# Two graph-attention layers, eight batches: rows of two stages spread by TensorE instead of through memory, exponentials issued ahead of the next normalisation, and a regrouped opening and ending

## What is computed

```python
h = relu(layernorm(x))                     # over the 128 features
Wh = h @ W                                 # [1024, 128]
e[i, j] = leaky_relu(Wh[i] @ a1 + Wh[j] @ a2, slope 0.2)
att = softmax over j of where(adj[i, j] > 0, e[i, j], -large)
x = x + elu(att @ Wh)                      # layer 0
x = x + att @ Wh                           # layer 1, with its own W and a
```

## Time and profile before

| | |
|---|---|
| median of 3 executions | 315.14 us (313.93 to 317.64) |
| profiled execution, its own time | 314.74 us |
| its span in the trace | 312.9 us |
| TensorE matmul busy | 293.6 us, 94% of the span |
| VectorE / ScalarE / GpSimd busy | 267.3 / 164.5 / 47.6 us |
| row_r from memory, 15 loads | 3.9 us each from issue to landing, median |

### The profile page before, as it was taken

How to read it: one execution, slowest core, us unless ns; L and a number is a source line. 1 busy time by engine, 2 the same in 40 slices (tenths; PEclk the granted TensorE clock), 3 DMA queues, 4 the chain that set the end, 5 groups by cost and what they waited for, 6 DMA issues and landing times.

```text
span 312.9 us, 6581 instructions
## 1 busy us (share of the span) xinstructions
PE 293.6 (94%) x2560; PEld 288.6 (92%) x2560; DVE 267.3 (85%) x610; ACT 164.5 (53%) x485; POOL 47.6 (15%) x53
## 2 busy tenths in 40 slices
PE   7999779799899999999999999999999999789695
PEld 7899679799899999999999999999999999788595
DVE  4596389949999989999899989999899959919785
ACT  3284480784493747483583648382674654353200
POOL 2612001220303030303003030303002000400000
PEclk9999999999999999999999999999999999999999
DMA  7997495102574334904574345713491302001211
GB/s 248 410 405 317 154 389 197 67 2 68 190 244 175 138 134 151 384 7 142 195 310 162 138 135 189 284 68 115 161 356 47 138 0 70 0 0 40 96 69 67
DMA packets 15247, 50.56 MB, mean 162 GB/s; under 512 B 2040, under 2 KB 3056, under 8 KB 15216
## 3 DMA queue, kind: packets, MB, share of 16 engines
q1 hardware_dynamic: 14640, 49.75, 43.0%
q10 hardware_dynamic: 576, 0.39, 0.4%
HBM read 45.88 MB, written 4.26 MB: 160 GB/s over the span
## 4 chain that ended last, share of the span: by engine, by line
PE 74%; DVE 10%; DMA 4%; ACT 4%; issue 4%; POOL 2%; POOLq 0%; DVEq 0%; ACTq 0%
PE acc L790 55%; PE prj L750 7%; PE tp L693 4%; DVE pbuf L564 4%; DMA row_r<-r_rows 3%; PE acc L806 2%; PE acc L690 2%; ACT xn L349 2%; POOL rstd L254 2%; DMA r_rows<-rT 1%; DVE stats L476 1%; DVE x_sb L594 1%; DVE ex L588 1%; PE prj L753 1%; DVE accs L573 1%
## 5 line engine op out<-in xcount | busy, mean ns | idle before, releaser
L790 PE MATMUL acc<-wh,pbuf 128*128 128x129 f32 x1984 | 232.9, 276 | 10.1 <-DVE accs L573 8.1
L790 PEld LDWEIGHTS acc<-wh,pbuf 128*128 128x128 f32 x1984 | 227.0, 192 | 13.3 <-issue 9.9
L564 DVE SCALAR_TENSOR_TENSOR pbuf<-row_r,sqr,adj_sb 128x1024 f32<-128x1024 f32 x127 | 157.8, 1278 | 8.8 <-DMA row_r<-r_rows 8.8
L254 POOL TENSOR_TENSOR rstd<-vareps,neg_half 128x8 f32<-128x8 f32 x15 | 37.5, 2503 | 213.9 <-DVE vareps L494 213.8
L379 ACT ACTIVATE accs<-accs,rec 128x128 f32<-128x128 f32 x120 | 36.7, 390 | 59.3 <-DVE rec L583 59.3
L349 ACT ACTIVATE xn<-x_sb,shift,rstd 128x128 f32<-128x128 f32 x120 | 47.6, 480 | 0.0
L368 ACT ACTIVATE wh<-prj,wh 128x128 f32<-128x128 f32 x120 | 31.6, 350 | 0.0
L750 PE MATMUL prj<-w_ext,hT 128*128 128x130 f32 x240 | 29.4, 275 | 0.1
L750 PEld LDWEIGHTS prj<-w_ext,hT 128*128 128x128 f32 x240 | 28.0, 191 | 0.2 <-ACT hT L355 0.2
L573 DVE TENSOR_TENSOR accs<-acc,uniform 128x387 f32<-128x387 f32 (+1 forms) x48 | 22.0, 508 | 4.2 <-PE acc L790 2.0
L476 DVE BATCH_NORM_STATS2 stats<-x_sb 128x6 f32<-128x128 f32 x120 | 24.6, 279 | 0.0
(11 more groups left out here) (81 smaller groups left out, 146.1 us busy)
## 6 DMA issues: line engine op xcount, KB each, us to landing
adj_sb<-in_adj SPq DMA_DIRECT2D x64, 512.0 KB, 6.5
row_r<-r_rows SPq DMA_DIRECT2D x15, 512.0 KB, 3.9
x_sb<-in_x SPq DMA_DIRECT2D x7, 512.0 KB, 7.1
out_x<-x_sb SPq DMA_DIRECT2D x7, 512.0 KB, 3.0
out_x<-x_sb SPq DMA_DIRECT2D x2, 192.0 KB, 1.9
x_sb<-in_x ACTq DMA_DIRECT2D x1, 256.0 KB, 3.6
x_sb<-in_x SPq DMA_DIRECT2D x1, 256.0 KB, 3.4
r_rows<-rT SPq DMA_DIRECT2D x15, 4.0 KB
```

The source lines that it names most:

```text
L254: nc.gpsimd.tensor_tensor(rstd[:, :], vareps[:, :], neg_half[:, :], ALU.pow).then_inc(rstd_ready, 1)
L564: nc.vector.scalar_tensor_tensor(pbuf[:, t, :], row_r[:, n % 2, :], sqr[:, n % 2, 0, t:t + 1], adj_at(b, t), ALU.max, ALU.min).then_inc(p_ ...
L790: mm = nc.tensor.matmul(acc[:, k, s * C:(s + 1) * C], pbuf[:, t, i * P:(i + 1) * P], wh[:, n % 2, t, :], start=(t == 0 and s == 0), stop=( ...
```

## The change

1. **Rows of stages 1 and 15** (`SPREAD`) no longer go through memory. TensorE spreads them by 8 transposes (`spread_r`) in the place of `turn_r`, and ScalarE copies them to `row_r` in two halves (`copy_row`). The mask tiles of batch 2 are issued without a wait for row 1, and x of batches 4 and 5 goes behind `load_row(2)`.
2. **ScalarE's order.** In the stage before a LATE one, `copy_hT(n+1)` goes ahead of `scale_accs(n-1)`, and `exps(n+1)` with the row's copy ahead of `normalise(n+2)`. In stage 0 `normalise(2)` goes ahead of `exps(1)`. The very first exponentials are split: row values first, the two others after them.
3. **Opening.** Warm-up counts 24, 6, 4, 3 become 20, none, 2, 3 (the second entry of the new tuple is not used). W a of layer 0 is computed after the first four transposes, that of layer 1 after the first projection. Six of the eight statistics of batch 1 are issued ahead of `copy_e_first`, two behind it.
4. **VectorE's order.** The masks issued ahead of `take_acc` are 4 for stage 1, 1 for stage 3, 3 for stage 13 and 2 otherwise. The statistics of stages 3, 5 and 15 are moved: those of 3 and 15 ahead of the mask tiles 7 and 6 to 7 of the stage before, those of 5 from the head of stage 3 to the place behind `exp_args(4)`.
5. **TensorE's order around LATE stages.** In stage 2 `transposes(3)` follows two tiles instead of one, then one tile, then `project(3)`; in stage 14 `transposes(15)` follows one tile, then one tile, then `project(15)`. In stages 1 and 13 `turn_r` stands one tile later.
6. **Ending.** The last output tile goes to a bank of its own (`LAST_TILE`, in `prj`), which ScalarE first fills with the `uniform` row (`seed_last`); the ending has four parts (3, 3, 1 and 1 tiles), and the last is read from PSUM without a copy.

```diff
+    SPREAD = (1, LAST)
+    last_parts = [(0, NB), (NB, 2 * NB), (2 * NB, T - 1), (T - 1, T)]
+        LAST_TILE = prj[:, 0, 0:C]
+        def before_drain(n):
+            return {1: 4, AHEAD: 1, LAST - 2: 3}.get(n, 2)
...
@@ SyncE
-            for m in range(1, AHEAD):
-                for t in range(T):
-                    load_adj(m, t)
-                load_x(m + 2)
-                load_row(m)
-                sp.wait_ge(row_in, 16 * m)
-            load_x(AHEAD + 2)
+            for t in range(T):
+                load_adj(1, t)
+            load_x(3)
+            for t in range(T):
+                load_adj(2, t)
+            load_row(2)
+            load_x(4)
+            load_x(5)
             load_row(AHEAD)
...
@@ ScalarE
+            def copy_row(m):
+                k = spread_rows(m)
+                for h in range(2):
+                    act.wait_ge(row_spread, 2 * k + h + 1)
+                    cols = slice(h * (N // 2), (h + 1) * (N // 2))
+                    nc.scalar.activation(row_r[:, m % 2, cols], tp[:, cols],
+                                         ACT.Copy).then_inc(row_copied, 1)
+            def seed_last():
+                act.wait_ge(wh_ready, T * LAST + T)
+                act.wait_ge(e_copied, 3 * LAST + 3)
+                nc.scalar.activation(LAST_TILE, uniform[:, LAST % 2, :],
+                                     ACT.Copy).then_inc(seeded_last, 1)
...
+            normalise(2)
+            exps(1)
+            scale_wh(1, range(3))
+            copy_row(1)
+            scale_wh(1, range(3, T))
+            copy_hT(2)
+            for n in range(1, LAST + 1):
+                elu = stages[n - 1][0] == 0
                 if n + 1 in LATE:
                     copy_hT(n + 1)
+                scale_accs(n - 1)
+                if n + 1 in LATE or n + 2 in LATE:
                     elu_exp(n - 1) if elu else None
+                if n < LAST:
                     exps(n + 1)
+                    if n + 1 in SPREAD:
+                        copy_row(n + 1)
+                    else:
+                        copy_r(n + 1)
+                    if n + 1 not in LATE and n + 2 not in LATE:
+                        elu_exp(n - 1) if elu else None
+                    if n + 2 <= LAST and n + 2 not in LATE:
+                        normalise(n + 2)
                     scale_wh(n + 1)
                 if n + 2 in LATE:
                     normalise(n + 2)
                 elif n + 2 <= LAST:
                     copy_hT(n + 2)
+            seed_last()
...
@@ TensorE
+            def spread_r(m):
+                pe.wait_ge(sqr_ready, m + 1)
+                for t in range(T):
+                    mm = nc.tensor.transpose(tp[:, t * P:(t + 1) * P],
+                                             sqr[:, m % 2, 2, t:t + 1].to_broadcast([P, P]),
+                                             ident[:, :])
+                    if t % 4 == 3:
+                        mm.then_inc(row_spread, 1)
...
+                        if t == 0 and n == LAST and i == T - 1:
+                            pe.wait_ge(seeded_last, 1)
...
                 if n + 1 in LATE:
-                    attend(n, (0,))
+                    k = 1 if n + 1 in SPREAD else 2
+                    attend(n, range(k))
                     transposes(n + 1)
-                    attend(n, (1, 2))
+                    attend(n, (k,))
                     project(n + 1)
-                    attend(n, (3,))
+                    attend(n, (k + 1,))
                     spread_emax(n + 1)
-                    attend(n, (4,))
-                    turn_r(n + 1)
-                    attend(n, (5,))
+                    attend(n, (k + 2,))
+                    spread_r(n + 1) if n + 1 in SPREAD else turn_r(n + 1)
+                    attend(n, range(k + 3, 6))
                 else:
                     project(n + 1)
                     attend(n, (0,))
                     spread_emax(n + 1)
-                    attend(n, (1,))
+                    attend(n, (1, 2) if n + 2 in LATE else (1,))
                     turn_r(n + 1)
-                    attend(n, (2, 3, 4, 5))
+                    attend(n, (3, 4, 5) if n + 2 in LATE else (2, 3, 4, 5))
                 if n + 2 <= LAST and n + 2 not in LATE:
                     transposes(n + 2)
                 attend(n, (6, 7))
```

More of the change, by code:

```diff
@@ L160, in gat_two_layers @@
         x1_ready = sem("x1_ready")
+        seeded_last = sem("seeded_last")
         last_ready = sem("last_ready")
@@ L172, in adj_at, with spread_rows, loaded_rows @@
             return adj_sb[:, s:s + N]
+        def before_drain(n):
+            return {1: 4, AHEAD: 1, LAST - 2: 3}.get(n, 2)
+        def spread_rows(m):
+            return len([k for k in SPREAD if k < m])
+        def loaded_rows(m):
+            return len([k for k in range(1, m + 1) if k not in SPREAD])
         def xn_before(m):
@@ L363, in exps, with scale_wh @@
                 nc.scalar.mul(wh[:, m % 2, :, D], sqr[:, m % 2, 1, :], Q_SCALE).then_inc(q_ready, 1)
-            def scale_wh(m):
+            def scale_wh(m, tiles=range(T)):
                 act.wait_ge(q_ready, m + 1)
-                for t, (k, s) in enumerate(bank_of):
+                for t in tiles:
+                    k, s = bank_of[t]
                     nc.scalar.activation(wh[:, m % 2, t, 0:D], prj[:, k, s * E:s * E + D],
@@ L409, in _ @@
             scale_wh_first(range(T - 1, T))
[L410 to L413, removed]
+            normalise(2)
[6 more added lines that the diff above has]
+                elu = stages[n - 1][0] == 0
                 if n + 1 in LATE:
                     copy_hT(n + 1)
+                scale_accs(n - 1)
+                if n + 1 in LATE or n + 2 in LATE:
                     elu_exp(n - 1) if elu else None
-                    normalise(n + 2) if n + 2 <= LAST else None
+                if n < LAST:
                     exps(n + 1)
[L419 to L428, removed]
-                if n < LAST:
+                    if n + 1 in SPREAD:
[6 more added lines that the diff above has]
+                        normalise(n + 2)
                     scale_wh(n + 1)
@@ L464, in statistics_first, with statistics_second @@
                                             ALU.add, ALU.max).then_inc(xn_dve, 1)
+            def statistics_second(tiles):
+                src = x3_at(1)
+                if tiles[0] == 0:
+                    dve.wait_ge(x_in[1], 16)
+                    dve.wait_ge(vareps_ready, 1)
+                    nc.vector.memset(gate[:, :], 0.0)
+                for t in tiles:
+                    st = nc.vector.bn_stats(stats[:, t, :], src[:, t, :])
+                if tiles[-1] == T - 1:
+                    st.then_inc(bn_done, 1)
             def statistics(m):
@@ L641, in _ @@
                 l, b = stages[n - 1]
-                if n + 2 <= LAST and n + 2 not in LATE and n + 1 not in LATE:
+                if n + 2 <= LAST and not {n, n + 1, n + 2} & set(LATE):
                     statistics(n + 2)
                     moments(n + 2)
-                masks(n, (0, 1))
+                masks(n, range(before_drain(n)))
                 take_acc(n - 1)
@@ L678, in _ @@
                     masks(n, (6, 7))
-            masks(LAST, (0, 1))
+            masks(LAST, range(before_drain(LAST)))
             take_acc(LAST - 1)
@@ L836, in _ @@
             attend(0, (4,))
-            turn_r(1)
+            spread_r(1)
             attend(0, (5, 6))
```

194 lines of the change are left out of this document (129 added, 65 removed).

## The result

The changed kernel takes 305.81 us (median of 4, 305.2 to 306.9); the kernel before took 314.53 beside it. The ratio is 0.9709, 95% interval 0.9664 to 0.9754. The profiled execution of the changed kernel took 305.33 us with a span of 303.5. Forecast were 303.9 and a span of 301.7.

The account below looks back on a forecast made before the run. TensorE, busy 94%, bounds the kernel; only its waits in stages 1-3 and 13-15 can go. Stage 4 -6.1, stages 13 and 14 -2.1 - 4.5, seed +2.1, ending -0.6: -11.2, giving 303.9 us, range 299.8 to 307.8.

Parts of the forecast that it names:

- norms come late: Rival, chance 0.17: opening gives nothing, shifts locked out in stages 3 and 13 (+0.9), `exps(1)` waits 0.8; 306.6 us.
- Opening: Before stage 0: fewer first transposes and split exponentials start stage 0 1.7 us earlier, 1.0 of it kept.
- the rival of the slow clock: Rival, chance 0.03: TensorE stays at 1.2 GHz into stage 0; a whole stage 0 so would give 321 us.
- The old waits of 1.95 and 2.98 us: TensorE's waits before stages 1 and 15, where VectorE's masks waited for the row from memory; forecast to go.
- the rival by which VectorE's own work keeps them: Rival, chance 0.05: in stages 1 and 15 VectorE's work replaces the row as bound, both waits stay; about 309 us.
- lands at 47.6: Stage 1: row 2, written at 42.5, lands at 47.6, before VectorE is ready for it at 47.8.
- First new wait: Stage 2: TensorE waits 2.0 us at `transposes(4)`, since ScalarE does stage 3's exponentials and row copy before `normalise(4)`.
- 1.6 us given back by the sum: Stage 3: moved statistics of stage 5 delay mask 3 (+1.1 with the handover), and the accumulators come late (+0.5).
- the first free gap: Stages 3 and 14: GpSimd's shift gets in at the first gap among VectorE's masks; otherwise 0.2 and 0.7 late.
- The 0.5 that I had put on the accumulators of stage 3: Start of stage 4: VectorE takes stage 3's accumulators from 91.9, TensorE comes at 92.0 and starts at 92.5, +0.5.
- Second new wait: Stage 15, first tile: TensorE waits 2.0 to 2.1 us for `seed_last`, issued by ScalarE behind `scale_accs(14)`.
- Stages 13 and 14, ending: Stages 13 and 14 gain 2.1 and 4.5 us as old waits go; the smaller last part gains 0.6.

Follow-up runs that it names:

- five repairs: Changed kernel with seed, transposes and statistics repairs, stage 2's second mask behind the accumulators, x of batches 4 and 5 ahead of row 2: 299.38 us.
- three repairs: Changed kernel with the seed ahead of the scaling, stage 4's transposes one tile later, stage 5's statistics at the head of stage 3: 299.42 us.
- second experiment: Changed kernel with the transposes of stage 4 one tile later in stage 2: 304.91 us.
- third: Changed kernel with the statistics of stage 5 back at the head of stage 3: 304.82 us.
- sixth experiments: Changed kernel with VectorE waiting in stage 3 for GpSimd's shift of stage 5, before the addition: 306.08 us.

## Why the prediction was right

The two new waits, the old ones that go and the stages that don't change came as worked out. The time did not fall in the likeliest band, 302 to 305.5: 305.81 lies 0.3 above it, where the prediction had put the rival "norms come late" (305.5 to 308.5, chance 0.17). Of that rival's three parts one came, in stage 3: a shift held up beside VectorE's instructions, which cost 1.43 us there and had been priced at 0.2. The opening did gain, and `exps(1)` cost TensorE 0.35 us, not 0.8.

- **The order of reading.** The 17.40 us of a middle stage were untouched (156.59 us for nine stages, before and after), and all of the gain and all of the losses lie in stages 0 to 3 and 13 to 15.
- **Opening.** Forecast 1.7 at stage 0, measured 1.47; 1.0 kept at `transposes(1)`, measured 1.21. The clock rose near 7 with 20 transposes as with 24. Leaving them out costs 1.9 at stage 0, so the rival of the slow clock had a true mechanism, but even with no warm-up it cost 1.9 us, not the 11.2 that it needed.
- **The rows.** Stage 1 starts 0.1 from the forecast. The old waits of 1.95 and 2.98 us are gone, and undoing each half brings one back (4.76 and 3.29 us in the profiles, 7.8 and 1.5 us in the medians). So the rival by which VectorE's own work keeps them is wrong. I had not priced the clock, which is part of the 7.8.
- **Row 2.** The step "lands at 47.6" failed by 0.9: with x of two batches behind it in the queue the read took 4.5 us, not the median of 3.9; with x ahead of it, as with five repairs, it took 3.4. It became 0.34 at stage 2 and some tenths before it. In other executions the write of row 2 takes 1.9 to 2.9 us, and the step is off by up to 2.6.
- **First new wait.** Forecast 2.0 for the norm of stage 4, measured 1.83; moving the transposes by a tile takes it away.
- **Stage 3.** This is the term that was mis-sized: 1.6 us given back by the sum, against the 2.4 us of the two waits. The mask wait was forecast at 1.1 and measured 1.01. The norm wait was put at 0 (0.2 by the rule), and is 1.43. I took "the first free gap" for the shift; it did not get in between the third mask and the addition, but at the next boundary, between the addition and mask 6, though no gap is there either. The Trainium skill ("SBUF — State Buffer", "Who interferes with whom") has the rule that an instruction of VectorE with two SBUF inputs contends with a GpSimd instruction that reads SBUF. The trace agrees (2.02 us; 0.88 with a gap), and the addition counts as well as a mask, which I had not taken into account. Why that one boundary was missed is open. The 0.5 that I had put on the accumulators of stage 3 vanished in it.
- **Second new wait.** Forecast 2.0 to 2.1 for the seed, measured 1.86; issuing it earlier removes it. The step stood on the order of ScalarE's queue alone.
- **Stages 13 and 14, ending.** 14.57 and 18.20 us against 14.6 and 18.35. The shift of stage 15 took 0.88 and not 2: it ended at 263.69, between the third and the fourth of four masks, and `transposes(15)` had no wait. Here "the first free gap" was right. From the start of stage 15 to the end it is 19.8 us, against 19.7 forecast. VectorE and GpSimd:

```profile
259.96 4.86 DVE L655 SCALAR_TENSOR_TENSOR pbuf<-row_r,sqr,adj_sb 128x1024 f32<-128x1024 f32 x4
```

```profile
262.81 0.88 POOL L284 TENSOR_TENSOR shift<-negmean,rstd 128x8 f32<-128x8 f32 x1
```

What is left open: why the 4 KB write of a row takes 1.2 us in some executions and up to 2.9 in others. Traffic of mask tiles does not explain it: in the execution of the three repairs the DMA engines moved 7 GB/s during the write (stretch, us, TensorE busy, granted clock, DMA share, GB/s). The kernel before is another case: there the write of row 2 took 5.0 us while the engines moved 324 GB/s, against 1.2 us and 16 GB/s in the changed kernel's profile. Issuing the tiles of batch 2 earlier took them out of this write's way.

```profile
43.00:46.00 3.00, 3.00 (x29) 1.00 0.03 7
```

## What to carry to other kernels

When a bound engine waits for a moved or added instruction on another one, walk that engine's own queue: both new waits (1.83 and 1.86 us measured) could be read off the order of ScalarE's instructions, and both went away by moving one call. Put a producer in a queue where its inputs are ready, not where its output belongs; and count work that only has to be in time ahead of a drain by what delays it, since each mask ahead of the accumulators hands a late row on to TensorE. A chain over GpSimd that falls into a run of VectorE instructions with two SBUF inputs, additions as well as masks, waits for one or two of them: the `shift` got in at the end of the one that was running in stage 15 (0.88 us) and only at the end of the next one in stage 3 (2.02 us). It did not have to wait for the end of the run, which goes on to 87.7. Price both cases, or leave a gap where the chain is on TensorE's path.

## What the runs showed of the hardware

The wait costs more than its length. After idle stretches of 1.86 us at the seed TensorE kept its 2.4 GHz in some executions (the changed kernel's profile) and fell to 1.2 GHz in others: the windows of the second experiment above read 0.86 and 0.50. After 4.76 us it had fallen in the profile shown. The mean granted clock that goes with each execution says how often. With the seed's wait it was 0.994 in one of 4 executions of the changed kernel (306.9 us; the others 305.2 to 306.3) and in 7 of 12 of the second, third and sixth experiments, and 0.999 in the one without warm-up; without the wait it was 0.998 or more in all 20 executions of the four kernels that issue the seed early. In the two traces with 0.994 the drop stands right behind the seed. One count speaks against a simple rule: with the row of stage 15 through memory the profiled execution idles 3.29 us and, 1.8 us later, 1.79 us for the seed, the clock granted behind both is 1.00, and all four executions have a mean of 0.998 or 0.999. What decides is not shown. Of the 31 executions of the kernel before that were made beside the experiments, the six with a mean of 1.000 took 313.1 to 314.7 us, the others, with 0.987 to 0.995, 314.0 to 317.9. The two overlap, so the clock is not all of it. The spread also went from 1.7 us in the changed kernel to 0.3 in the last one (2.7, 2.1 and 1.0 in the other three that issue the seed early); that the waits made it wide is argued, not shown.
